# A gated delta rule kernel with its diagonal 8x8 blocks inverted on GpSimd, denser q and k tiles, and a rewritten order of work

## The chip, the cores and the metric

One core of a Trainium2 chip runs the whole program. The metric is the device time of one execution in microseconds (us), the median of the runs shown. Lower is better. TensorE is called PE here, VectorE DVE, ScalarE ACT, GpSimd POOL and SyncE SP, as the profile calls them.

## What is computed

The reference is one block of a network on x of 8 batches, 256 tokens and 256 features: a modulated layer norm, a gated delta rule attention with 32 heads, a gated feed forward, then a second modulated layer norm and a mixture of 8 experts. Nearly all of the time goes to the attention, cut here to what matters:

```python
q = short_conv(h @ Wq, conv_q_w).reshape(b, t, H, DK)    # H = 32, DK = 48
k = short_conv(h @ Wk, conv_k_w).reshape(b, t, H, DK)
v = short_conv(h @ Wv, conv_v_w).reshape(b, t, H, DV)    # DV = 96
q, k = (l2norm(q), l2norm(k))
g = -jnp.exp(A_log) * jax.nn.softplus(h @ Wa + dt_bias)
beta = jax.nn.sigmoid(h @ Wb)
def step(S, inp):                                        # over the tokens
    qt, kt, vt, gt, bt = inp
    S = S * jnp.exp(gt)[..., None, None]
    mem = jnp.einsum('bhk,bhkv->bhv', kt, S)
    delta = (vt - mem) * bt[..., None]
    S = S + jnp.einsum('bhk,bhv->bhkv', kt, delta)
    return (S, jnp.einsum('bhk,bhkv->bhv', qt * scale, S))
gate = (h @ Wg).reshape(b, t, H, DV)
o = (rmsnorm(o, gnorm_w) * jax.nn.silu(gate)).reshape(b, t, VD) @ Wo
```

short_conv is a causal convolution of 4 taps for each feature, followed by silu.

## The kernel before

The program has three parts, one after the other: `prepare` (norms, decay factors, beta), `delta_rule` (the attention) and `experts`. The change touches `delta_rule`, and `prepare` a little.

**Items.** `delta_rule` works on 64 items: 8 groups of 4 heads (QH = 4) times 8 batches. An item has two chunks of 128 tokens (CH = 2), so 8 units (U = 8) of one head and one chunk. In a chunk the recurrence becomes a linear system with a unit triangular matrix of 128 by 128 for each unit; the kernel inverts that matrix and then solves with two rounds of refinement (REFINE = 2).

**Inversion.** Seven levels (LEVELS = 7) join blocks of 1, 2, 4, ... 64 to blocks of twice the size. A level has two halves g = 0, 1 of 4 units each. `merge1(l, g)` multiplies the transposed inverse so far (tile tn) with the matrix (tile b16) on PE (L521), and DVE masks the result (L711, tile w16). `merge2(l, g)` makes the next tn (PE L534, ACT L840) and the next inverse tt (PE L541, ACT L843). The first and the last level need no L534. All four matmuls of a half are 128x128 in bf16.

**Stages.** An item passes four turns. Stage A makes q, k, v (`qk`, `v`, `taps`), the gates, the row norms (`norms`, `gains`), the decays (`decays`: 8 scans of 128 on DVE, L734), the key tile (`keys`), and the triangular matrices (`scores` on PE, `decayed` on DVE, `negate` on ACT and POOL). Stage B is the inversion, in all 14 halves of a turn. Stage C is the solve (`w0`, then `residual` and `delta` in turn, `state_out`, `ks`), and its end (`gated`, `oT`, `wo`, `acc`) reaches into the next turn as stage D. In one turn A, B, C and D work on four different items.

**Order.** A turn has 15 slots. `slots` walks through them and calls, on every engine, the pieces in one written order: merge2 and merge1 of B, then the tables A_FIRST, C_AT, D_AT and A_AT. Each engine executes its own instructions in that order and waits on semaphores for the others. So an instruction that waits holds everything queued behind it on its engine. POOL has the squares, two power functions, the scaled key tile kqb, and two `affine_select` for each chunk. SP issues, for each item, a copy of h (tile hb, L491), the decays (L492) and the cumulative decays (L495), and once in 8 items the weights.

q and k lie in 4 tiles of 128 rows, in which each head of 48 takes 64 rows (the rest is zero), so that a head starts at row 0 or 64.

Of the kernel before, what the change touches and what calls it, by code (L numbers as in the profile page):

```python
# [14 lines left out]
TAPS = 4  # L15
# [6 lines left out]
QH = 4  # L22
# [3 lines left out]
VT = QV // P  # L26
STEPS = NQ * B
U = CH * QH
LEVELS = 7
# [12 lines left out]
C_ID, C_MASK, C_HEAD, C_IOTA = 0, P, P * (1 + LEVELS), P * (1 + LEVELS) + 2  # L42
C_COLS = C_IOTA + E
# [58 lines left out]
def prepare(nc, A, mem, scr):  # L102

    with ExitStack() as ctx:
# [32 lines left out]
        z_ps, absz_ok, u_ok, sp_ok, a_ok, eb_ok, beta_ok, bt_ps, bcum_ok = (  # L137
            sem(n) for n in ("z_ps", "absz_ok", "u_ok", "sp_ok", "a_ok", "eb_ok", "beta_ok", "bt_ps", "bcum_ok"))
# [6 lines left out]
        def _(sp):  # L145
# [18 lines left out]
            sp.wait_ge(a_ok, 1)  # L164
            for g in range(GROUPS):
                sp.dma_start(scr["a"][2 * g:2 * g + 2].rearrange("b h t -> h b t"),
                             tmp["a"][H * g:H * (g + 1), :].rearrange("h (b t) -> h b t", b=2)).then_inc(scr_st, 16)
# [41 lines left out]
        def _(pool):  # L209
            pool.memset(nh[:], -0.5).then_inc(half_ok, 1)  # L210
            pool.wait_ge(half_ok, 1)
            def turn(g):
# [31 lines left out]
        def _(v):  # L244
# [4 lines left out]
            v.tensor_copy(mem["id16"][:], const[:, C_ID:C_ID + P])  # L249
            v.tensor_copy(mem["mask"][:], const[:, C_MASK:C_MASK + LEVELS * P].rearrange("p (l n) -> p l n", l=LEVELS))  # L250
# [84 lines left out]
def delta_rule(nc, A, mem, scr):  # L335

    with ExitStack() as ctx:
# [41 lines left out]
        cj = sb("cj", [P, QH])  # L379
# [37 lines left out]

        C_AT = {0: [("w0", 0)], 1: [("residual", 0, 0)], 2: [("delta", 0, 0)], 3: [("residual", 0, 1)],
# [1030 lines left out]
```

## Time and profile before

| what | value |
|---|---|
| median of 3 runs | 2803.08 us (2802.49 to 2806.18) |
| the profiled execution, its own time | 2806.17 us |
| its span in the profile | 2804.3 us, 61239 instructions |
| PE busy | 2561.5 us, 91% |
| PE weight loads busy | 2142.8 us, 76% |
| DVE busy | 2278.5 us, 81% |
| ACT busy | 1757.5 us, 63% |
| POOL busy | 597.0 us, 21% |
| mean granted clock of PE | 0.969 |

The loop of `delta_rule` runs from about 131 us to 2475 us of the span. Shares over the whole span therefore mix the loop with the parts around it; the loop is better read in a window of its own. A run of matmuls is shown as busy until its last result has come out, while the next run may start earlier, so the busy time of PE is more than the time in which it could take no other work.

### The profile page before, as it was taken

How to read it: one execution, taken by the hardware profiler on the slowest of the kernel's cores; microseconds unless marked ns; L12 is line 12 of the kernel's file. 1: busy time of each engine (PE TensorE's matmuls, PEld its weight loads, DVE VectorE, ACT ScalarE, POOL GpSimd, SP SyncE). 2: the span in 40 equal slices, each digit the busy share in tenths (PEclk: the TensorE clock that was granted, in tenths of full speed). 3: DMA queues.
4: the chain of work that ended last, by engine and by line, in shares of the span. 5: the costliest groups of instructions: out<-in, count | busy, mean ns of one | idle time of the engine just before them, and what ended most of it. 6: DMA issues, size and time to landing. Idle time of an engine off the chain costs nothing. (4 is left out here: it accounts for less than half of the span.)

```text
span 2804.3 us, 61239 instructions
## 1 busy us (share of the span) xinstructions
PE 2561.5 (91%) x22496; PEld 2142.8 (76%) x22496; DVE 2278.5 (81%) x5647; ACT 1757.5 (63%) x4018; POOL 597.0 (21%) x733
## 2 busy tenths in 40 slices
PE   1279999999999999999999999999999999879997
PEld 0168888888888888888888888888888888746565
DVE  3469999999999999999999999999999999624444
ACT  1157777777777777777777777777777777622221
POOL 0022222222222222222222222222222222100000
PEclk6589999999999999999999999999999999989998
DMA  2310011001100010002000200020002000030000
GB/s 92 94 41 28 14 45 41 28 15 32 54 25 18 23 50 28 28 8 64 28 28 2 71 28 28 2 71 28 28 2 71 28 28 1 1 114 26 12 24 15
DMA packets 93542, 95.34 MB, mean 34 GB/s; under 512 B 31217, under 2 KB 82106, under 8 KB 93250
## 3 DMA queue, kind: packets, MB, share of 16 engines
q1 hardware_dynamic: 93250, 91.44, 10.6%
q8 instruction: 184, 3.01, 0.4%
q14 instruction: 108, 0.88, 0.1%
HBM read 72.10 MB, written 2.54 MB: 27 GB/s over the span
## 5 line engine op out<-in xcount | busy, mean ns | idle before, releaser
L711 DVE TENSOR_TENSOR dr_w<-dr_ps,mask 128x512 bf16<-128x512 f32 x768 | 522.3, 680 | 175.3 <-PE dr_ps L521 175.2
L725 DVE SCALAR_TENSOR_TENSOR dr_y<-dr_ps,dr_cw,dr_y 128x255 f32<-128x255 f32 (+2 forms) x1344 | 573.0, 473 | 28.5 <-ACT dr_y L850 21.9
L840 ACT CAST dr_tn<-dr_ps 128x512 bf16<-128x512 f32 x640 | 374.9, 586 | 153.1 <-PE dr_ps L534 153.1
L843 ACT CAST dr_tt<-dr_ps 128x512 bf16<-128x512 f32 x768 | 460.5, 600 | 1.4 <-PE dr_ps L541 1.4
L625 PE MATMUL dr_ps<-dr_w,dr_am 128*128 128x96 f32 x3072 | 417.3, 279 | 2.5 <-ACT dr_w L902 2.5
L625 PEld LDWEIGHTS dr_ps<-dr_w,dr_am 128*128 128x128 f32 x3072 | 377.9, 192 | 10.5 <-ACT dr_w L902 3.0
L541 PE MATMUL dr_ps<-dr_tt,dr_w 128*128 128x128 bf16 x3072 | 297.9, 219 | 69.4 <-DVE dr_w L711 69.4
L521 PE MATMUL dr_ps<-dr_tn,dr_b 128*128 128x128 bf16 x3072 | 297.1, 219 | 0.0
L534 PEld LDWEIGHTS dr_ps<-dr_w,dr_tt 128*128 128x128 bf16 x2560 | 186.4, 98 | 141.3 <-issue 70.0
L547 PE MATMUL dr_ps<-dr_hb,dr_wqk 128*128 128x256 f32 x1024 | 255.8, 394 | 22.1 <-DMA dr_hb<-hT 22.1
L541 PEld LDWEIGHTS dr_ps<-dr_tt,dr_w 128*128 128x128 bf16 x3072 | 204.2, 98 | 81.3 <-DVE dr_w L711 80.6
L534 PE MATMUL dr_ps<-dr_w,dr_tt 128*128 128x128 bf16 x2560 | 249.0, 220 | 7.1 <-DVE dr_w L711 5.9
L944 POOL TENSOR_TENSOR dr_sq<-dr_qk 128x256 f32<-128x256 f32 x128 | 78.4, 612 | 718.2 <-ACT dr_qk L860 718.2
L734 DVE TENSOR_TENSOR_SCAN dr_dec<-dr_abc,const 128x128 f32<-128x128 f32 x512 | 223.5, 497 | 0.0
L547 PEld LDWEIGHTS dr_ps<-dr_hb,dr_wqk 128*128 128x128 f32 x1024 | 188.3, 194 | 43.7 <-issue 22.4
L767 DVE SCALAR_TENSOR_TENSOR dr_am<-dr_ps,dr_gam,dr_dec 128x256 f32<-128x256 f32 x512 | 216.8, 474 | 3.0 <-PE dr_ps L608 2.9
L968 POOL TENSOR_TENSOR dr_fo<-dr_vo,dr_nhalf 128x4 f32<-128x4 f32 x128 | 130.2, 1017 | 400.1 <-DVE dr_vo L805 400.1
L960 POOL TENSOR_SCALAR_AFFINE_SELECT dr_b<-dr_b 128x512 bf16<-128x512 bf16 x128 | 94.5, 738 | 546.2 <-ACT dr_b L892 546.2
L521 PEld LDWEIGHTS dr_ps<-dr_tn,dr_b 128*128 128x128 bf16 x3072 | 203.9, 98 | 0.0
L547 PE MATMUL dr_ps<-dr_hb,dr_wv 128*128 128x256 f32 x768 | 198.0, 394 | 0.8 <-DVE dr_y L725 0.8
L902 ACT COPY dr_w<-dr_ps 128x384 f32<-128x384 f32 x384 | 188.5, 491 | 12.0 <-PE dr_ps L625 11.9
L690 PE MATMUL dr_ps<-dr_wo,dr_oT 128*128 128x256 f32 x768 | 194.5, 390 | 1.0 <-ACT dr_oT L928 1.0
(187 smaller groups left out, 4688.8 us busy)
## 6 DMA issues: line engine op xcount, KB each, us to landing
dr_abc<-scr_a SPq DMA_DIRECT2D x64, 512.0 KB, 4.1
dr_hb<-hT SPq DMA_DIRECT2D x64, 256.0 KB, 2.5
dr_bcb<-scr_b SPq DMA_DIRECT2D x128, 64.0 KB, 3.3
ex_modb<-scr_mod SPq DMA_DIRECT2D x4, 1024.0 KB, 8.1
dr_wo<-in_Wo SPq DMA_DIRECT2D x1, 3072.0 KB, 11.3
dr_wv<-in_Wv SPq DMA_DIRECT2D x8, 384.0 KB, 4.1
dr_wg<-in_Wg SPq DMA_DIRECT2D x8, 384.0 KB, 4.0
p_x<-in_x SPq DMA_DIRECT2D x4, 512.0 KB, 6.3
```

The lines of the kernel that those rows point to most:

```text
L521: last = pe.matmul(ps[:, (X0, X1)[g], (u % QH) * P:(u % QH + 1) * P], b16[:, m, u, :], id16[:] if l == 0 else tn[:, u, :], start=True, sto ...
L534: last = pe.matmul(ps[:, (X2, X1)[g], (u % QH) * P:(u % QH + 1) * P], tt[:, u, :], w16[:, u, :], start=True, stop=True)
L541: last = pe.matmul(ps[:, (X0, X2)[g], (u % QH) * P:(u % QH + 1) * P], wt[:, u, :], id16[:] if l == 0 else tt[:, u, :], start=True, stop=True)
L547: last = pe.matmul(ps[:, bank, off:off + T], wt(k), hb[:, m, k, :], start=(k == 0), stop=(k == KT - 1))
L625: last = pe.matmul(ps[:, bank, h * DV:(h + 1) * DV], wt(h), x[:, h * DV:(h + 1) * DV], start=(start and h == 0), stop=(h == QH - 1), skip_ ...
L690: last = pe.matmul(ps[:, CO, 0:D], oT[:, t, :], wo[:, (it // B) * VT + t, :], start=(t == 0), stop=(t == VT - 1))
L711: v.tensor_tensor((tn if l == 0 else w16)[:, us, :], ps[:, (X0, X1)[g], :].rearrange("p (u n) -> p u n", u=QH), bc(mask[:, l, :], 1, QH), ...
L725: v.scalar_tensor_tensor(y[:, slot, x:T], ps[:, (A0, A1)[n % 2], off:off + T - x], cw[:, t, TAPS - 1 - x:TAPS - x], y[:, slot, x:T], ALU.m ...
L734: v.tensor_tensor_scan(dec[:, u, :], abc[:, m, h, c * P:(c + 1) * P], ident, 0.0, ALU.mult, ALU.add).then_inc(s["dec_ok"], 1)
L767: ins = v.scalar_tensor_tensor(am[:, m, u], ps[:, (A0, A1)[side], a * 2 * P:(a + 1) * 2 * P].rearrange("p (n t) -> p n t", n=2), gam[:, m, ...
L840: act.copy(tn[:, us, :], ps[:, (X2, X1)[g], :].rearrange("p (u n) -> p u n", u=QH)).then_inc(s["tn_ok"], 1)
L843: act.copy(dst, ps[:, (X0, X2)[g], :].rearrange("p (u n) -> p u n", u=QH)).then_inc(s["tt_ok"], 1)
```

## The change

1. **Inversion.** LEVELS goes from 7 to 4: the levels now start from blocks of 8. The inverses of the 8x8 diagonal blocks are made by forward substitution on POOL (`base`): one copy and 14 small dependent operations on 128 x (8 x 7 down to 8 x 1) elements. SP copies the diagonal 16x16 blocks of b16 into a dense tile (8 DMAs per item, `blocks`), PE spreads their rows with 14 bf16 matmuls of 64 columns (`rows`), ACT copies the result (128x448), POOL solves, and DVE expands the 8x8 results to full 128x128 tiles tt and tn (`expand`: a product, a 32x32 transpose and two products of 128x1024 in bf16). All levels but the last now make a new tn.
2. **Order.** The inversion starts at position 27 of an item's life (slot 12 of the second turn) and ends at 35 (slot 5 of the third); the solve starts at 36 (slot 6 of the third turn) where it started at 30. Slots 6 to 11 of a turn hold no merge, and `expand` lies in slot 11.
3. **Dense tiles.** q and k together take 3 tiles of 128 rows (KTL = 3) in place of 4. The convolution runs over 6 tiles in place of 7. After silu, SP moves the 8 heads to the old places by 10 DMAs per item (`heads_apart`). h is read in place, so the copy hb is gone.
4. **Scans.** The decay scans are 2 of 512 elements per item in place of 8 of 128. Their second input is now a diagonal times the gain gam, made on POOL (tile dg, two products of 128x512), so that the gain is in the decay. `decayed` is then 4 products of 128x512 in place of 8 of 128x256 with a scalar.
5. **Moved.** The scaling of the key tile goes from DVE to ACT (a copy) and POOL (`keys_scale`). The output norm factor is multiplied into the gate on POOL (2 products of 128x384 per item), and `gated` is 1 product of 128x384 per chunk in place of 4 of 128x96.

The core of the diff:

```diff
-LEVELS = 7
+BASE = 8
+LEVELS = 4
+LVL0 = 3
+M_FIRST = 27
+DEPTH = 4
...
+        FIRST = {3: [("silu", 0)], 5: [("silu", 1)], 7: [("silu", 2)], 11: [("negate", 0)], 13: [("negate", 1)]}
+        SOLVE = {36: [("w0", 0)], 37: [("residual", 0, 0)], 38: [("delta", 0, 0)], 39: [("residual", 0, 1)],
+                 40: [("delta", 0, 1)], 41: [("state_out",)], 42: [("ks",), ("mean", 0)], 43: [("w0", 1)],
+                 44: [("residual", 1, 0), ("gated", 0)], 45: [("delta", 1, 0), ("oT", 0)],
+                 46: [("residual", 1, 1), ("wo", 0)], 47: [("delta", 1, 1), ("acc", 0)], 48: [("out", 1)],
+                 49: [("mean", 1)], 51: [("gated", 1)], 52: [("oT", 1)], 54: [("wo", 1)], 55: [("acc", 1)]}
+        BLOCKS = {17: [("values", 0)], 18: [("round", 0)], 19: [("values", 1)], 20: [("rows", )], 21: [("base",)],
+                  26: [("expand",)]}
+        MAKE = {0: [("proj", 0)], 1: [("taps", 0, 0)], 2: [("taps", 0, 1), ("proj", 1)],
+                3: [("taps", 1, 0)], 4: [("taps", 1, 1), ("proj", 2)], 5: [("taps", 2, 0)],
+                6: [("taps", 2, 1), ("norms",)], 7: [("gains",), ("gate", 0)],
+                8: [("keys",), ("gate", 1)], 9: [("scores", 0), ("decays", 0)],
+                10: [("decayed", 0, 0), ("decayed", 0, 1), ("keys_scale",)], 11: [("scores", 1), ("decays", 1)],
+                12: [("decayed", 1, 0), ("decayed", 1, 1)]}
+        SLOTS = 15
...
+            for half in range(SLOTS):
+                at = [(st, half + SLOTS * k) for k, st in enumerate(stages) if st]
+                for st, x in at:
+                    k = x - M_FIRST
+                    if 0 < k <= 2 * LEVELS:
+                        on["merge2"](st, (k - 1) // 2, (k - 1) % 2)
+                    if 0 <= k < 2 * LEVELS:
+                        on["merge1"](st, k // 2, k % 2)
+                for table in (FIRST, SOLVE, BLOCKS, MAKE):
...
+            def expand(st):
+                it, m = st
+                v.wait_ge(s["xb_ok"], it + 1)
+                v.tensor_tensor(c32[:].rearrange("p u (r i) -> p u r i", r=4), bc(xb[:], 2, 4),
+                                bc(bc(const[:, C_QUART:C_QUART + 4], 1, U), 3, BASE), ALU.mult).then_inc(s["c32_ok"], 1)
+                v.wait_ge(s["c32_ok"], it + 1)
+                v.transpose(c32t[:].rearrange("p u i -> p (u i)"), c32[:].rearrange("p u i -> p (u i)")
+                            ).then_inc(s["c32t_ok"], 1)
...
+                v.tensor_tensor(tt[:].rearrange("p u (n i) -> p u n i", i=4 * BASE), bc(c32[:], 2, 4), blk,
+                                ALU.mult).then_inc(s["te_ok"], 1)
+                v.wait_ge(s["c32t_ok"], it + 1)
+                v.tensor_tensor(tn[:].rearrange("p u (n i) -> p u n i", i=4 * BASE), bc(c32t[:], 2, 4), blk,
+                                ALU.mult).then_inc(s["te_ok"], 1)
...
                 pe.wait_ge(s["rs_ok"], (it * 2 + 1) * REFINE)
+                pe.wait_ge(s["kg_ok"], it + 1)
...
+            def base(st):
+                it, m = st
+                n = it * (2 * BASE - 2)
+                wait(pool, s["c32_ok"], it)
+                pool.tensor_copy(xb[:], bc(const[:, C_UNIT:C_UNIT + BASE], 1, U)).then_inc(s["xs"], 1)
+                pool.wait_ge(s["ab_ok"], it + 1)
+                for j in range(BASE - 1):
+                    left = BASE - 1 - j
+                    pool.wait_ge(s["xs"], n + 2 * j + 1)
+                    pool.tensor_tensor(xt[:, :, 0:left], bc(xb[:, :, j], 2, left), ab[:, j, :, j + 1:BASE],
+                                       ALU.mult).then_inc(s["xs"], 1)
+                    pool.wait_ge(s["xs"], n + 2 * j + 2)
+                    ins = pool.tensor_tensor(xb[:, :, j + 1:BASE], xb[:, :, j + 1:BASE], xt[:, :, 0:left], ALU.add)
```

On POOL the order in a turn is, after the change: squares (slot 3), the scaling of the gate (4), `base` (6), then in slot 7 the two products dg, the square root of the norms and kqb, `keys_scale` (10), the selects (11 and 13) and again the scaling of the gate (12).

## Rows read from the trace of the kernel before

**Rows 1.** Busy time of each engine in one stretch of the loop (columns: stretch, length, PE, PEld, DVE, ACT, POOL, PEclk, DMA).
```profile
600.00:1000.00 400.00, 386.63 (x3750) 338.81 (x3748) 363.17 (x897) 291.47 (x674) 100.16 (x123) 1.00 0.11 33
```
**Rows 2.** Who waited for whom, whole span (total us, times, longest).
```profile
DVE dr_w L711 <- PE dr_ps L521: 175.2, 200, 3.6
```
**Rows 3.** Two lines of DVE (ns min/median/max, first and last start).
```profile
L734 DVE TENSOR_TENSOR_SCAN dr_dec<-dr_abc,const x512: 393/401/794, 138.8 to 2410.1; 128x128 f32<-128x128 f32 x171
...
L742 DVE TENSOR_SCALAR dr_kk<-dr_ps x64: 153/155/166, 149.0 to 2397.8; 128x8 f32<-128x8 f32 x64
```
**Rows 4.** Timeline of PE, single pieces (columns: start, us shown busy, instructions).
```profile
1005.99 1.46 PE L586 MATMUL dr_ps<-dr_wg,dr_hb 128*128 128x384 f32 x4
...
1007.28 0.39 PE L534 MATMUL dr_ps<-dr_w,dr_tt 128*128 128x128 bf16 x4
...
1007.51 0.39 PE L541 MATMUL dr_ps<-dr_tt,dr_w 128*128 128x128 bf16 x4
...
1010.31 1.08 PE L625 MATMUL dr_ps<-dr_w,dr_am 128*128 128x96 f32 x8
...
1011.23 1.49 PE L690 MATMUL dr_ps<-dr_wo,dr_oT 128*128 128x256 f32 x6
...
1019.99 1.96 PE L547 MATMUL dr_ps<-dr_hb,dr_wqk 128*128 128x256 f32 x8
```
**Rows 5.** Groups of DVE by form, 1000 to 1400 us (count, busy us, mean ns, idle before).
```profile
L711 DVE TENSOR_TENSOR dr_w<-dr_ps,mask 128x512 bf16<-128x512 f32 x134 | 91.1, 680 | 28.9 <-PE dr_ps L521 28.9
...
L725 DVE SCALAR_TENSOR_TENSOR dr_y<-dr_ps,dr_cw,dr_y 128x254 f32<-128x254 f32 x79 | 37.4, 474 | 0.4
L767 DVE SCALAR_TENSOR_TENSOR dr_am<-dr_ps,dr_gam,dr_dec 128x256 f32<-128x256 f32 x88 | 37.3, 474 | 0.0
...
L783 DVE TENSOR_TENSOR dr_r<-dr_rhs,dr_ps 128x384 bf16<-128x384 f32 x45 | 24.7, 548 | 5.0 <-PE dr_ps L625 5.0
L813 DVE SCALAR_TENSOR_TENSOR dr_og<-dr_ps,dr_fo,dr_gs 128x96 f32<-128x96 f32 x89 | 21.9, 307 | 0.0
```
**Rows 6.** Groups of DVE by form, 2400 us to the end.
```profile
L1368 DVE TENSOR_TENSOR ex_yo<-ex_yo,ex_x 128x1024 f32<-128x1024 f32 x4 | 4.9, 1226 | 0.1
```
**Rows 7.** Timeline, the handover from DVE to PE behind a mask.
```profile
1020.80 0.68 DVE L711 TENSOR_TENSOR dr_tn<-dr_ps,mask 128x512 bf16<-128x512 f32 x1
...
1021.78 0.39 PE L541 MATMUL dr_ps<-id,dr_tn 128*128 128x128 bf16 x4
```
**Rows 8.** Groups of ACT by form, 1000 to 1400 us.
```profile
L843 ACT CAST dr_tt<-dr_ps 128x512 bf16<-128x512 f32 x135 | 81.0, 600 | 0.0
L840 ACT CAST dr_tn<-dr_ps 128x512 bf16<-128x512 f32 x112 | 65.6, 586 | 26.0 <-PE dr_ps L534 26.0
```
**Rows 9.** Groups of POOL by form, 1000 to 1400 us.
```profile
L968 POOL TENSOR_TENSOR dr_fo<-dr_vo,dr_nhalf 128x4 f32<-128x4 f32 x23 | 23.4, 1017 | 64.6 <-DVE dr_vo L805 64.6
L950 POOL TENSOR_TENSOR dr_nrm<-dr_kk,dr_half 128x8 f32<-128x8 f32 x12 | 19.6, 1636 | 19.6 <-DVE dr_kk L742 19.6
L954 POOL TENSOR_TENSOR dr_kqb<-dr_qk,dr_bcb 128x256 f32<-128x256 f32 x24 | 17.0, 732 | 0.0
...
L944 POOL TENSOR_TENSOR dr_sq<-dr_qk 128x256 f32<-128x256 f32 x22 | 13.5, 612 | 119.6 <-ACT dr_qk L860 119.6
```
**Rows 10.** Timeline, the scans of the two chunks and POOL beside the first shown.
```profile
1014.40 2.14 DVE L734 TENSOR_TENSOR_SCAN dr_dec<-dr_abc,const 128x128 f32<-128x128 f32 x4
...
1014.73 0.84 POOL L960 TENSOR_SCALAR_AFFINE_SELECT dr_b<-dr_b 128x512 bf16<-128x512 bf16 x1 [8.01 <-ACT dr_b L892]
...
1026.76 1.36 DVE L734 TENSOR_TENSOR_SCAN dr_dec<-dr_abc,const 128x128 f32<-128x128 f32 x4
```
**Rows 11.** Busy time and granted clock in the second turn (columns as in the first group).
```profile
191.90:195.30 3.40, 1.34 (x18) 0.93 (x15) 3.40 (x8) 2.15 (x4) 0.72 (x2) 1.00 0.33 94
195.30:198.70 3.40, 3.32 (x19) 2.99 (x20) 1.96 (x5) 1.59 (x3) 1.22 (x2) 0.50 0.52 178
```
**Rows 12.** DMA issues by line (count, KB each, median us to landing).
```profile
dr_hb<-hT SPq DMA_DIRECT2D x64, 256.0 KB, 2.5
```

More of the change, by code:

```diff
@@ L26, with head_rows @@
 VT = QV // P
+QK = QH * DK
+KTL = 2 * QK // P
+def head_rows():
+    out = []
+    for n in range(2):
+        for h in range(QH):
+            at, end = n * QK + h * DK, n * QK + (h + 1) * DK
+            while at < end:
+                rows = min(end, (at // P + 1) * P) - at
+                out.append((n, h, at - n * QK - h * DK, at // P, at % P, rows))
+                at += rows
+    return out
+HEAD_ROWS = head_rows()
 STEPS = NQ * B
 U = CH * QH
-LEVELS = 7
+BASE = 8
[3 more added lines that the diff above has]
+DEPTH = 4
 REFINE = 2
@@ L423, in delta_rule @@
-        A_AT = {0: [("qk", 0)], 1: [("taps", 0, 0)], 2: [("taps", 0, 1), ("qk", 1), ("decays", 0)],
-                3: [("taps", 1, 0)], 4: [("taps", 1, 1), ("v", 0)], 5: [("taps", 2, 0)],
-                6: [("taps", 2, 1), ("norms",), ("v", 1)], 7: [("gains",), ("taps", 3, 0), ("gate", 0)],
-                8: [("keys",), ("gate", 1)], 9: [("scores", 0)], 10: [("decayed", 0, 0), ("decayed", 0, 1)],
-                11: [("scores", 1), ("decays", 1)], 12: [("decayed", 1, 0), ("values", 0)],
-                13: [("decayed", 1, 1), ("round", 0)], 14: [("values", 1)]}
@@ L449, in delta_rule @@
         PIECES = ("merge1", "merge2", "w0", "delta", "residual", "ks", "out", "state_out", "mean", "gated", "oT", "wo",
-                  "acc", "qk", "qk_silu", "v", "v_silu", "taps", "gate", "norms", "gains", "decays", "keys", "scores", "decayed", "negate",
+                  "acc", "rows", "base", "expand", "proj", "silu", "taps", "gate", "norms", "gains", "decays", "keys", "keys_scale", "scores", "decayed", "negate",
                   "values", "round")
@@ L569, in norms @@
+                for j in range(2):
+                    t = 2 * n + j
+                    for k in range(KT):
+                        wt = wqk[:, k, t * P:(t + 1) * P] if t < KTL else wv[:, k, (t - KTL) * P:(t - KTL + 1) * P]
+                        last = pe.matmul(ps[:, BANK[n], j * T:(j + 1) * T], wt, hT[:, k, (it % B) * T:(it % B + 1) * T], start=(k == 0),
+                                         stop=(k == KT - 1))
+                last.then_inc(s["pj_ps"], 1)
             def norms(st):
@@ L692, in wo_ @@
                 last.then_inc(s["wo_ps"], 1)
-            on.update(merge1=merge1, merge2=merge2, qk=qk_, v=v_, norms=norms, gate=gate, keys=keys, scores=scores,
+            on.update(merge1=merge1, merge2=merge2, rows=rows_, proj=proj, norms=norms, gate=gate, keys=keys, scores=scores,
                       values=values, w0=w0, residual=residual, delta=delta, out=outputs, state_out=state_out, ks=ks,
```

412 lines of the change are left out of this document (225 added, 187 removed).

## The prediction

> **What bounds the kernel now.** I read the busy time in a stretch of the loop first, since shares over the whole span mix in the parts around it. In 400 us PE is busy 387 us, DVE 363, ACT 291 and POOL 100, at a granted clock of 1.00 [rows 1]. The item's line L742 gives the turn: (2397.8 - 149.0) / 63 = 35.7 us [rows 3]. So a turn holds 34.5 us of PE as shown, 32.4 of DVE, 26 of ACT and 9 of POOL.
>
> Next, what of PE's time is real. Two runs of four bf16 matmuls start 0.23 us apart and are shown busy 0.39 us each [rows 4]: a matmul of 128 columns costs 0.056 us, and 0.16 us of each shown run is the last result coming out. By the same deduction a projection of eight instructions costs 1.75 us (L547), a gate chunk 1.3 (L586), a wo chunk 1.3 (L690) and a product of four heads in fp32 0.9 (L625) [rows 4]. Over the pieces of a turn this gives 33 us of PE that can't overlap. The waits agree: the largest wait of DVE is L711 for PE, 175 us, 2.7 us a turn [rows 2]. So PE (33) and DVE (32.4) are each nearly full, and about 2.7 us of 35.7 are lost because both execute one written order and hold each other up. The queue order matters as much as the sums.
>
> **The sums after the change, per turn.**
> - PE: merges go from 152 matmuls to 88, -64 x 0.056 = -3.6. One projection tile of seven goes, -0.87; norms -0.4 (12 small matmuls for 16, estimated at 0.11); `rows` adds 14 matmuls of 64 columns, below 0.056 each, +0.6. 33 becomes about 28.8.
> - DVE: six masks less, -6 x 0.68 = -4.1 [rows 5]. Three taps less, -1.4. `gated` goes from 8 x 0.31 to 2 x 0.55, -1.4; `decayed` from 8 x 0.47 to 4 x 0.68, -1.1; the keys leave, -0.6. The eight scans take 1.36 + 2.14 = 3.5 [rows 10]; two of 512 cost 1.1 to 1.36 each, because one element follows the other, about -1.1. `expand` is new. Its two products of 128x1024 lie between 0.68 (the rate of two elements in the time of one; nearest row L711, half as long) and 1.23 each (L1368, fp32) [rows 5, 6]; with the small product and the transpose, 2.0 to 3.2, and I take 2.5, about the middle, since the form isn't in the trace. 32.4 becomes about 25.
> - ACT: ten copies of 0.59 less [rows 8], some small work gone, two copies added: about 20.
> - POOL: the two dg products (two inputs, 512 elements) cost up to twice kqb's 0.73, I take 1.3 each; the gate scalings about 1.0 each; the key scaling 0.7 [rows 9]. For each of `base`'s 14 operations the rows give bounds: 0.61 for 256 elements, so 0.08 for the mean of 32 if the time were all per element, and above that a fixed part between 0 and 0.4 (1.64 - 1.02 = 0.62 us for four elements more of the power, so 1.02 has 0.4 fixed) [rows 9]. `base` lies between 1.3 and 7 us; with 0.2 of fixed part and handover I take 4. POOL has 9 + 2.6 + 2.0 + 0.7 + 4 = 18 us.
>
> No engine sum exceeds 29. If sums decided, the turn would fall by 4 to 6 us. They don't, and this is the step on which I depend.
>
> **The walk through the new order.** Before, each slot held a merge, which gives PE and DVE equal work. Now slots 6 to 11 have none, and DVE gets `expand`, the 512 scan and the state copy in one slot. I follow the loop of dependencies from PE's `merge2(0,1)` in slot 14 to the same instruction a turn later.
>
> Stretch 1, PE in order from there to `scores(0)` in slot 9: 72 merge matmuls 4.0, three projections 5.25, two gates 2.6, two wo 2.6, four residuals 3.6, the second output 1.55, scores 1.0, three deltas and a w0 0.7, the transposes 1.5, norms 1.3, rows 0.6. Sum 24.7 us. DVE can't prepare stretch 3 meanwhile: its queue stands at `decayed(0)`, which needs these scores.
>
> Stretch 2, scores to S: `delta(0,1)` 0.2, ACT's copy of w 0.5, the state product 0.5, three handovers 0.5. Sum 1.7.
>
> Stretch 3, DVE's queue from the state copy: copies 0.75, `expand` 2.5, scan 1.15, mask 0.6, the ks subtraction 0.46, `mean` 0.65, two `decayed` 1.25, mask 0.65: 8.0 us (an operation starts some 0.08 before its predecessor's shown end: four scans of 0.40 take 1.36 [rows 3, 10]). PE has only about 2.7 us of work beside it, in pieces that wait for these results, and its next instruction needs the last mask. Handover to a weight load behind a mask: 1021.78 - 1021.48 = 0.3 [rows 7].
>
> That is 24.7 + 1.7 + 8.0 + 0.3 = **34.7 us without one stall in stretch 1**. This floor moves with `expand` from 34.2 to 35.4.
>
> Stalls in stretch 1. (a) `norms`: the second projection ends 5.7 us of PE work before PE comes to norms, but its chain is ACT copy 0.85, taps 1.2, mask 0.65, mean 0.68, values 0.5, taps 1.2 on DVE, then two silus and a square 1.6, and handovers 0.6: 7.4. (Each is a count of operations at the rates of these groups [rows 5, 8], less the 0.08 of overlap; silu and square I take at 0.4 for 256 elements.) Stall 1.8. (b) The first merges and `oT(0)` behind DVE: 0.8. (c) `gate(1)` needs the bank that ACT reads, and little is queued between now: 0.5. Sum 3.1.
>
> (d) A wait is added: `state_out` waits for kg_ok. What is queued behind it on PE is the output product, scores(1), the first merge and ks; DVE's copy of S waits for it. On POOL, kg stands behind `base`, dg x2 2.6, nrm 1.64, kqb 1.46 and itself 0.7, that is 6.4 after `base`. `base` starts when ACT has copied the rows, behind silu(1), 0.6 us before norms can start; the state product could start 10 us after that. With `base` 4: 10.4. Stall 0.4; each us of `base` above 3.6 adds one us to the turn.
>
> Turn: 34.7 + 3.1 + 0.4 = **38.2 us**, 2.5 more than now. For 62 full turns +155. Around the loop: 8 fewer small weight DMAs and no copy of h (2.5 us to landing [rows 12]), against a later store of the decays and six more slots of drain; I take 0, bounds -10 and +10. The heads' 10 DMAs are hidden: the last three land, at the 2.5 us of L491 behind 1.8 of issue, about when `keys` is reached; if a us late, the turn grows by that us. The 8 DMAs of blocks have five slots of cover. The profiled execution took 2806.2, 3 above the median 2803.1; so 2806 + 155 = 2961, for the median **2958 us**.
>
> **A rule weighed.** The first scans run beside POOL's select and take 2.14 us for four, the others, alone, 1.36 [rows 10]: 0.39 for each of two held scans. By the Trainium skill, page "SBUF — State Buffer", section "SBUF: two separate sides", the shared port pair is an exclusive lock between GpSimd and a VectorE operation with two SBUF inputs, held for the whole instruction. The row agrees in sign and size. It speaks against this change, which doubles POOL's work and gives DVE three more operations of that kind: by it the turn could be 39.8, by the walk alone it is 38.2.
>
> **The rivals.**
> - *The port.* Five operations of DVE per turn (two scans, three of `expand`) have two SBUF inputs; four lie in stretch 3. At 0.4 each [rows 10] the turn is 39.8 and the time 3058. For it: POOL is busy half of the turn. Against: by my walk it is idle when `expand` runs. (Its page is the one just named.) 8%.
> - *The clock.* PE has 4 us of work in 11 us of stretches 2 and 3. In the second turn now, a stretch of 3.40 with PE busy 1.34 us was followed by one at a granted 0.50, that is 1.2 GHz in place of 2.4 [rows 11]. If this happens in every turn and the slow stretch falls on the start of stretch 1, 3.4 us give 1.7 us of work: turn 39.9, 3064. Against: the loop now is at 1.00, and the place can shift. 20%.
> - *POOL's chain.* `base` at 7 us adds 3: 41.2, 3144. 7%.
> - *The other side: faster.* The stalls of stretch 1 vanish since ACT and DVE slide ahead where I let them wait. It decides at 1.0 us: with stalls below that, 34.7 + stalls is under 35.7. With none and a short `expand`, 34.2: 2710; the middle of the case is 34.9, 2755. For it: now only 2.7 us are lost in a fuller turn. Against: the chain behind norms has 1.8 us more than PE has work. 25%.
> - *Nothing.* 35.6 to 35.8 us: 5%. This includes that the parts don't save what they say, for instance a scan of 512 that costs as much as four of 128.
>
> **How the numbers follow.** The walk 35%, slower: its own range is 36.9 to 39.4, 2877 to 3032. Port, clock and POOL, slower too: 35%. Faster 25%, nothing 5%. A measurement of this kernel can tell about 0.2% from no change. The range goes from 2725 (all of the faster case but its lowest tail) to 3110 (all but most of POOL's case). So faster 0.25, same 0.05, slower 0.70.
>
> **What would show it.** In the changed profile: a turn by L742's successor of 38.2; PE below 80% and DVE below 72% of a loop window; the largest waits being PE's first merge for te_ok and `merge2(0,1)` for its mask; a wait of norms for ACT's square. `expand` about 2.5 us, `base` about 4. The prediction fails if PE waits less than 5 us a turn, if `base` is over 5 or DVE's two-input operations stretch beside POOL, or if the granted clock is below 0.98 in the loop.

## The result and the profile after

| | before | after |
|---|---|---|
| median of 4 runs each | 2802.78 us | 3124.66 us (3124.19 to 3127.57) |
| ratio to before, 95% interval | | 1.1148 [1.1129, 1.1167] |
| span of the profiled execution | 2804.3 us | 3122.2 us |
| mean granted clock of PE | 0.969 | 0.871 |

The changed kernel is 11.5% slower: 322 us. The forecast was 2958 with a range up to 3110, so the direction was right, the size was not, and the time lies 15 us outside the range.

The page of after, its busy times and the granted clock in 40 slices of the span:

```profile
span 3122.2 us, 53272 instructions
...
PE 2577.8 (83%) x18784; PEld 2069.2 (66%) x18784; DVE 1969.4 (63%) x4176; ACT 1429.2 (46%) x3314; POOL 1187.9 (38%) x2027
...
PEclk6679988888888998888888888888888888879998
```

One eighth of the instructions is gone, DVE is busy 309 us less, ACT 328 less, and the program is longer. The row to see is PEclk: 8 in nearly every slice of the loop. A stretch of the loop as in [rows 1] (columns: stretch, length, PE, PEld, DVE, ACT, POOL, PEclk, DMA, GB/s), and the source line of `gains`, as in [rows 3]:

```profile
600.00:1000.00 400.00, 341.88 (x2707) 285.17 (x2705) 271.60 (x564) 203.47 (x479) 179.50 (x307) 0.88 0.14 31
```
```profile
L828 DVE TENSOR_SCALAR dr_kk<-dr_ps x64: 156/159/167, 143.6 to 2697.8; 128x8 f32<-128x8 f32 x64
```

In 400 us PE has 45 us less than in [rows 1] and DVE 92 less. (2697.8 - 143.6) / 63 = 40.5 us for a turn, where [rows 3] gave 35.7. Most turns of the steady loop (49 of 59) are 40.96 to 41.02 us long. Below, "a turn" is the mean of 59 turns of the loop between starts of this line (before 35.75, after 40.79), and "half-clock time" is what of a turn ran at a granted clock of 0.50.

Who waited for whom after the change, whole span (total us, times, longest):

```profile
DVE dr_r L857 <- PE dr_ps L691: 465.1, 254, 5.4
DVE dr_w L778 <- PE dr_ps L585: 350.5, 377, 3.9
...
PE dr_ps L598 <- DVE dr_w L778: 143.8, 130, 1.5
```

DVE's wait for its mask has doubled [rows 2], and its wait for the residuals of the solve is new in size. PE waits for DVE too. Both wait for each other: no engine is full.

**One turn by its stretches.** The order in time is: the pieces from the state copy to `merge2(0,1)` (here up to about 1001), then the long run of PE, the norms at 1022, gates and scores, and the state copy of the next turn at 1034.8:

```profile
996.00:1000.90 4.90, 2.28 (x24) 1.69 (x24) 4.83 (x8) 1.48 (x3) 1.29 (x2) 1.00 0.00 0
1001.00:1007.90 6.90, 6.19 (x42) 6.00 (x43) 3.06 (x6) 4.28 (x10) 2.01 (x3) 0.51 0.06 5
1008.00:1018.00 10.00, 10.00 (x95) 9.21 (x94) 7.05 (x16) 6.18 (x16) 0.54 (x1) 1.00 0.02 1
1018.00:1024.80 6.80, 5.18 (x54) 4.76 (x53) 5.67 (x14) 4.73 (x12) 4.37 (x11) 1.00 0.23 53
1024.90:1028.30 3.40, 3.40 (x13) 1.80 (x11) 0.94 (x5) 1.45 (x5) 2.85 (x10) 0.50 0.74 141
1028.30:1042.00 13.70, 10.03 (x79) 7.30 (x78) 10.47 (x18) 4.15 (x9) 8.17 (x8) 1.00 0.08 19
```

Two stretches of each turn of 40.96 us, together 10.2 us, run at a granted 0.50, that is 1.2 GHz in place of 2.4. The first follows 4.9 us in which PE was busy 2.28, and but for its first 0.7 us it lies on work that PE does without a pause. The second lies wholly on such work and follows the wait before the norms:

```profile
1022.33 1.48 PE L641 MATMUL dr_ps<-const,dr_sq 128*128 128x8 f32 x12 [1.62 <-ACT dr_sq L944]
```

Eight of the 59 turns have nearly the same waits and yet only 5.0 to 5.9 us at half clock, and they take 39.1 to 40.0 us. The next turn after the one above is of this kind: its 4.9 us are as poor in PE work as those above, and the clock stays at 1.00 behind them.

```profile
1037.00:1041.90 4.90, 2.28 (x24) 1.70 (x24) 4.83 (x9) 1.48 (x3) 1.30 (x2) 1.00 0.02 3
1042.00:1048.00 6.00, 4.98 (x49) 4.41 (x50) 3.15 (x6) 4.34 (x10) 2.14 (x4) 1.00 0.05 3
```

So such a place brings its stretch in most turns, not in all.

The end of the turn, where DVE sets the pace (timeline; start, us, instructions, idle before):

```profile
1034.78 0.73 DVE L864 COPY dr_S<-dr_ps 64x192 f32<-64x192 f32 x2
...
1035.54 0.43 DVE L784 TENSOR_TENSOR dr_c<-dr_xb,const 128x256 bf16<-128x256 f32 x1
...
1036.00 0.45 DVE L787 STREAM_TRANSPOSE dr_c32t<-dr_c 128x256 bf16<-128x256 bf16 x1
1036.37 0.65 DVE L791 TENSOR_TENSOR dr_tt<-dr_c,bd 128x1024 bf16<-128x1024 bf16 x1
1036.42 1.09 POOL L1044 TENSOR_SCALAR_AFFINE_SELECT dr_am<-dr_am 128x512 f32<-128x512 f32 x1
1036.94 1.12 DVE L794 TENSOR_TENSOR dr_tn<-dr_c32t,bd 128x1024 bf16<-128x1024 bf16 x1
1037.98 1.21 DVE L820 TENSOR_TENSOR_SCAN dr_dec<-dr_abc,dr_dg 128x512 f32<-128x512 f32 x1
...
1038.12 0.40 PE L585 MATMUL dr_ps<-dr_tn,dr_b 128*128 128x128 bf16 x4 [1.50 <-DVE dr_tn L794]
...
1042.90 0.40 PE L598 MATMUL dr_ps<-dr_w,dr_tt 128*128 128x128 bf16 x4 [1.50 <-DVE dr_w L778]
...
1043.65 0.64 POOL L1044 TENSOR_SCALAR_AFFINE_SELECT dr_am<-dr_am 128x512 f32<-128x512 f32 x1
```

From the state copy (1034.78) to `merge2(0,1)` (1042.90) it is 8.12 us; the expansion (L784 to L794) takes 2.52. PE waits 1.50 us for DVE twice here, and 0.75 us once between them (before `merge2(0,0)`, at 1039.98). One of the two products of one form takes 0.65 us and the other 1.12, while POOL's select beside it takes 1.09 where the same select takes 0.64 at 1043.65.

### The profile page after: what moved, and what is told of

The parts are those of the page before. It is cut to its first block and busy times, and to the rows that moved or that the text cites. A ratio compares the mean times of both kernels' runs of the same rounds, so it can differ in the third digit from the quotient of the medians.

```text
span 3122.2 us, 53272 instructions
## 1 busy us (share of the span) xinstructions
PE 2577.8 (83%) x18784; PEld 2069.2 (66%) x18784; DVE 1969.4 (63%) x4176; ACT 1429.2 (46%) x3314; POOL 1187.9 (38%) x2027
## 5 line engine op out<-in xcount | busy, mean ns | idle before, releaser
L778 DVE TENSOR_TENSOR dr_w<-dr_ps,mask 128x512 bf16<-128x512 f32 x512 | 353.3, 690 | 352.8 <-PE dr_ps L585 350.5
L808 DVE SCALAR_TENSOR_TENSOR dr_y<-dr_ps,dr_cw,dr_y 128x255 f32<-128x255 f32 (+2 forms) x1152 | 477.1, 472 | 24.8 <-ACT dr_y L924 24.8
L857 DVE TENSOR_TENSOR dr_r<-dr_rhs,dr_ps 128x384 bf16<-128x384 f32 x256 | 141.9, 554 | 465.1 <-PE dr_ps L691 465.1
L910 ACT CAST dr_tn<-dr_ps 128x512 bf16<-128x512 f32 x384 | 224.4, 584 | 221.5 <-PE dr_ps L598 221.0
L924 ACT ACTIVATE dr_y<-dr_ps,dr_cw 128x256 f32<-128x256 f32 x384 | 161.0, 470 | 255.7 <-PE dr_ps L630 255.7
L652 PE MATMUL dr_ps<-dr_wg,hT 128*128 128x384 f32 x512 | 276.1, 678 | 0.7 <-ACT dr_gs L950 0.7
L630 PE MATMUL dr_ps<-hT,dr_wqk 128*128 128x256 f32 x768 | 215.3, 422 | 22.8 <-DMA dr_cw<-in_conv_v_w 21.9
L913 ACT CAST dr_tt<-dr_ps 128x512 bf16<-128x512 f32 x384 | 229.1, 597 | 0.0
L630 PEld LDWEIGHTS dr_ps<-hT,dr_wqk 128*128 128x128 f32 x768 | 161.6, 227 | 45.1 <-issue 23.9
L630 PE MATMUL dr_ps<-hT,dr_wv 128*128 128x256 f32 x768 | 187.0, 380 | 2.4 <-DVE dr_y L808 2.4
```

The source lines that it names most:

```text
L630: last = pe.matmul(ps[:, BANK[n], j * T:(j + 1) * T], wt, hT[:, k, (it % B) * T:(it % B + 1) * T], start=(k == 0), stop=(k == KT - 1))
L652: last = pe.matmul(ps[:, A0, 0:QV], hT[:, k, at:at + P], wg[:, k, :], start=(k == 0), stop=(k == KT - 1))
L778: v.tensor_tensor(w16[:, us, :], ps[:, (X0, X1)[g], :].rearrange("p (u n) -> p u n", u=QH), bc(mask[:, l, :], 1, QH), ALU.mult).then_inc(s ...
L808: v.scalar_tensor_tensor(y[:, slot, x:T], ps[:, BANK[n], off:off + T - x], cw[:, t, TAPS - 1 - x:TAPS - x], y[:, slot, x:T], ALU.mult, ALU ...
L910: act.copy(tn[:, us, :], ps[:, (X2, X1)[g], :].rearrange("p (u n) -> p u n", u=QH)).then_inc(s["tn_ok"], 1)
L913: act.copy(dst, ps[:, (X0, X2)[g], :].rearrange("p (u n) -> p u n", u=QH)).then_inc(s["tt_ok"], 1)
```

## The experiments

The theory after this reading had two parts. **Order:** a turn is the walk through the written order, and the expansion in slot 11 stands on it. **Clock:** PE's low activity in the waits brings stretches at half clock, and these cost on top. Rivals: the low clock costs nothing, since PE waits anyway; and POOL's chain (`base`) sets the turn. The place of the expansion and the clock are tested first, alone and together.

### Expansion three slots earlier

```diff
-                  26: [("expand",)]}
+                  23: [("expand",)]}
```


> Changed kernel with one edit: expand stands at position 23 (slot 8) in place of 26 (slot 11), where DVE now idles 4.9 us waiting for a residual. Order theory (DVE's queue from the state copy to the mask of merge(0,1), 8.1 us, lies on the loop, expand's 2.5 us in it): the turn falls by 2.5 us, 3125 to about 2970. POOL theory (POOL's chain base, dg, nrm, kqb, kg sets the turn): no change, or slower if the port makes base longer. Clock theory alone (only the half clock costs): no change beyond what the clock does; half-clock time per turn would have to fall.

Measured: 2965.77 us, 1.0582 [1.0565, 1.0600], 159 us less than after; a turn of 38.30 with 7.1 us at half clock. PE's wait for `tn` before merge1(0,0) (1.50 us above) is gone, and so is the one of 0.75 before merge2(0,0). The wait for the last mask, before merge2(0,1), stays as it was:

```profile
1022.90 0.40 PE L598 MATMUL dr_ps<-dr_w,dr_tt 128*128 128x128 bf16 x4 [1.50 <-DVE dr_w L778]
```

This part of the order theory holds. Eight turns of this run had only 2.2 us of half-clock time, and these took 36.35 us. A line through all 59 turns gives 35.3 at no half-clock time: a first sign that clock and turn go together.

### Fillers: work for PE in its waits

The function `fill(n)` issues n bf16 matmuls of 512 columns whose result nobody reads; 20 per item, some 4.3 us of PE's time: 7 before merge1(0,0), 4 before merge2(0,0), 6 before the norms and 3 before state_out.

```diff
+            def fill(n):
+                for _ in range(n):
+                    pe.matmul(ps[:, X1, :], id16[:], mask[:].rearrange("p l n -> p (l n)"), start=True, stop=True)
...
...
+                        fill(7)
...
+                    fill(4)
...
+                fill(6)
...
+                fill(3)
```


> Changed kernel plus 20 matmuls of 512 columns in bf16 per item, whose results nothing reads, into a bank that is free in slots 6 to 13: 6 before norms, 3 before state_out, 7 before the first merge and 4 before the second, 4.3 us of PE work at full clock, nearly all in places where PE waits 0.6 to 1.6 us. Clock theory (half clock is granted 10.2 us per turn and each such us costs 0.31): the granted clock returns to 1.00 and the turn falls by up to 3.0 us, to about 2940. Rival (the low clock only falls where PE waits anyway and costs nothing): same time or up to 1 us per turn slower, 3125 to 3190.

Measured: 2914.01 us, 1.0389 [1.0372, 1.0406]. It is 211 us faster with more work, and nothing else is changed. A turn is 37.50 us, and 37.2 in those without half-clock time. The granted clock in the loop rose from 0.90 to 0.99 and the turn got shorter with more work in it. The rival that the low clock costs nothing is out.

### Both

> Both edits. If order and clock are two separate terms, they add: 3125 - 155 - 185 = about 2785, about the kernel before. If moving expand alone cures the clock, it is no faster than the first of the two alone, about 2970 or below; fillers that no longer find a wait would make it slower than 2785.

Measured: 2874.05 us, 1.0247 [1.0230, 1.0265]; 251 us less than after where the sum of the two is 370. All turns are 36.80 us long without half-clock time. So the clock was cured and the turn was still longer than expected. The trace shows where:

```profile
1026.09 1.69 PE L576 MATMUL dr_ps<-mask,id 128*128 128x512 bf16 x7
1027.61 0.39 PE L591 MATMUL dr_ps<-dr_tn,dr_b 128*128 128x128 bf16 x4
```

With the expansion early, PE does not wait before merge1(0,0) (L591 here), and the seven fillers now delay it. A smaller part of the missing 119 us was counted twice: the early expansion alone already lowers the half-clock time of a turn from 9.6 to 7.1 us. The same place in the kernel with the early expansion alone:

```profile
1017.62 1.14 PE L674 MATMUL dr_ps<-dr_qk 64*128 64x256 f32 x8
1018.69 0.40 PE L585 MATMUL dr_ps<-dr_tn,dr_b 128*128 128x128 bf16 x4
```

Filler work is free only in a wait that is still there.

### Without base

The inversion of the 8x8 blocks is left out: POOL copies the unit matrix, and the 14 small products and sums are not done.

```diff
-                for j in range(BASE - 1):
-                    left = BASE - 1 - j
...
-                    ins.then_inc(s["xb_ok"] if j == BASE - 2 else s["xs"], 1)
+                pool.tensor_copy(xb[:], bc(const[:, C_UNIT:C_UNIT + BASE], 1, U)).then_inc(s["xb_ok"], 1)
```


> Changed kernel without the 14 small operations of base on POOL (only its copy of unit rows stays, behind the same wait), so the 8x8 blocks are not inverted. POOL theory: POOL's chain gets 5.3 us shorter and the turn falls by 2 us or more, below 3000. Order theory: kg_ok comes at the same time as ACT's copy of w, so at most 0.3 us per turn, 3105 to 3125.

Measured: 3122.83 us (two executions), a turn of 40.75. POOL is busy 138 us of 400 in place of 178, and the time does not move. In this order POOL's chain hides completely.

### Fewer fillers, in the waits that are left

With the early expansion: 6 before the norms, 2 before state_out, 5 before merge2(0,1) into bank A1, none elsewhere.

```diff
+                if l == 0 and g == 1 and 5:
+                    pe.wait_ge(s["am_ok"], min(it + 2, STEPS) * 4)
+                    fill(5, A1)
```


> The expansion one turn's slot 8 (position 23) as before, and 13 filler matmuls instead of 20, only where the trace with the early expansion shows TensorE waiting: 6 before the norms (wait 1.6 us), 2 before state_out (0.6 us), 5 before merge2(0,1) (1.5 us, on bank A1), none before merge1(0,0) and merge2(0,0), where it doesn't wait. Clock-plus-order theory: over the turns of the run with the expansion alone, turn = 35.31 + 0.42 x half-clock us, so without half clock a turn is 35.3 us; the 20 fillers gave 36.80 at full clock since 7 to 11 of them (1.6 to 2.4 us) stood on the path. Against that run's 2874 a gain of 1.5 us x 62 = 92: 2782 us, ratio to before 0.992, faster than the kernel before. If the fillers left out were needed and one 3.4-us stretch at half clock per turn comes back: 36.7 a turn, 2870. If the residual rivals (port, GpSimd) set the turn and not the order, it stays at 2874.

Measured: 2806.46 us, 1.001 [1.0001, 1.0019]. All turns are 35.76 us long at full clock. The gain over the 20 fillers is 68 us where 92 were expected. The line through the turns of the early expansion alone gave 35.3 at no half-clock time; 0.45 us of that isn't reached. The reason is the added wait, seen below.

### Which place brings which low stretch

Fillers before the norms alone, and in slots 11 to 13 alone, in the changed kernel (expansion at 26).

> The changed kernel with 6 fillers per item before the norms alone, in a wait of 1.6 us. It tells which low stretch the granted clock answers to. If both places count for themselves (the 6.8 us at half clock behind the norms, the 3.4 us behind slots 10 to 14): the first goes, 3.4 us stay, turn 37.84 + 0.307 x 3.4 = 38.9, 3124.7 - 2.1 x 62 = 2995 us, clock about 0.94. If the slots 10 to 14 alone bring both: no change, 3120.

Measured: 3020.47 us, 1.0774 [1.0754, 1.0794] (three executions took 3019 to 3021 us; a fourth took 11187, which no trace explains); a turn of 39.18 with 6.6 us at half clock.

> The changed kernel with the 14 fillers of slots 11 to 13 alone (3 before state_out, 7 before merge1(0,0), 4 before merge2(0,0)), none at the norms. If both places count for themselves: 3.4 us at half clock go and 6.8 stay, turn 37.84 + 0.307 x 6.8 = 39.9, 3060 us, clock about 0.91. If the slots 10 to 14 alone bring both: about 37.5 a turn, 2915 us as with all 20.

Measured: 3048.35 us, 1.0874 [1.0856, 1.0892]; a turn of 39.62 with 5.5 us at half clock.

Each alone gives 104 and 76 us, both together 211. So both places count, but I had assigned them the wrong way round: with the norms filled, the 6.8 us stay and the 3.4 us go. They are not independent either: with the slots filled, 5.5 us stay and not 3.4. The trace of the run with the norms filled shows what comes ahead of the stretch that is left: 4.9 us with PE busy 2.66, in the slots 10 to 14.

```profile
993.80:998.70 4.90, 2.66 (x21) 1.82 (x21) 4.79 (x8) 0.89 (x2) 1.84 (x2) 1.00 0.01 3
998.80:1005.50 6.70, 5.49 (x45) 5.27 (x44) 4.04 (x9) 3.80 (x8) 3.03 (x4) 0.50 0.03 2
```

With the slots filled instead, all but one of the low stretches between 1000 and 1260 us begin 0.4 to 2.5 us after the norms' matmuls have begun.

The run with the norms filled has something better: two turns near its start (243.5 to 317.8) in which the changed order ran at full clock throughout.

```profile
243.50:317.80 74.30, 64.28 (x563) 52.55 (x564) 54.51 (x115) 41.43 (x99) 34.78 (x63) 1.00 0.13 30
```

Two turns are 74.3 us: 37.18 each (280.68 - 243.50). The fillers there lie in the wait before the norms and lengthen nothing: from the last work before them to the norms it is 1.62 us, as without them. Its marks, for the comparison with the walk:

```profile
259.58 0.40 PE L609 MATMUL dr_ps<-dr_w,dr_tt 128*128 128x128 bf16 x4 [1.50 <-DVE dr_w L791]
```
```profile
286.05 1.13 PE L686 MATMUL dr_ps<-dr_qk 64*128 64x256 f32 x8
...
296.76 0.40 PE L609 MATMUL dr_ps<-dr_w,dr_tt 128*128 128x128 bf16 x4 [1.50 <-DVE dr_w L791]
```
```profile
288.63 0.35 DVE L877 COPY dr_S<-dr_ps 64x192 f32<-64x192 f32 x1
```

So the clock costs 40.96 - 37.18 = 3.8 us of such a turn, for 10.2 us at half speed.

### Merges two slots earlier

The merges are spread over the slots in which PE has little to do, without any filler.

```diff
-M_FIRST = 27
+M_FIRST = 25
...
+                  23: [("expand",)]}
```


> The expansion at position 23 and the merges two slots earlier (first at 25, slots 10 to 14 and 0 to 3), no fillers. The solve stays at 36. Order theory: merges then lie in the slots where TensorE waits for VectorE and fill its gaps (0.6 and 1.5 us), but they put masks between the decayed products on VectorE, which delays scores(1) and the residuals. If the written order is what sets the turn, it moves by up to 1.5 us either way from 38.3: 2870 to 3060 us; a gain shows as a higher clock as well, since TensorE's gaps get smaller. If the clock's low stretch behind the norms is independent of it, 6.8 us at half clock remain.

Measured: 2849.94 us (2835.6 to 2857.3), 1.016 [1.0129, 1.0190], better than expected (2870 at best) and 116 us less than with the expansion alone. A turn is 36.40 with only 2.8 us at half clock, and 35.16 where it is 0.4; the 6.8 us of the last case did not stay. A line through the turns gives 35.25 us at no half-clock time, where that of the expansion alone gives 35.31. So the gain is the clock's: useful work in PE's gaps does what fillers do.

### The same with fillers, and one slot more

Merges at 25, 5 fillers before the norms, 2 before merge2(0,0), 5 before merge2(1,1), the merge of slot 14 in this order:

> Expansion at 23, merges from 25, and 12 fillers in the waits that the trace without fillers shows: 5 before the norms (1.35 us), 2 before merge2(0,0) (0.62 us), 5 before merge2(1,1) (1.50 us, bank A1, whose reader is by then done). Over the turns of the run without fillers the turn is 35.16 us where only 0.4 us stood at half clock. Clock theory: all turns go to 35.15 us at full clock; against the 35.76 us and 2806 us of the kernel with the merges at 27, 0.6 x 62 = 37 less: about 2768 us, ratio 0.987. If fillers stand on the path by up to 0.5 us a turn: 2800, ratio 0.998.

Measured: 2801.44 us, 0.9985 [0.9976, 0.9994], 35.64 us in most turns at full clock: the upper of the two values expected. Merges at 24:

> The same with the merges from 24 (slots 9 to 14 and 0 to 2) and 10 fillers (5 norms, 2 before merge2(0,0), 3 before merge2(2,0)). Order theory: one more slot of TensorE work beside the scores, one less beside the projections; the mask of merge(0,0) now stands before the keys' and scores' VectorE work. Expected within 1 us of a turn of 35.2: 2705 to 2830; it tells whether the turn still depends on the written order once the clock is full, or on TensorE's own work (then no change from the one at 25).

Measured: 2968.74 us, 1.0579 [1.0562, 1.0595], outside what I had expected. The trace shows a new wait:

```profile
1012.30 1.24 DVE L797 TENSOR_TENSOR dr_c<-dr_xb,const 128x256 bf16<-128x256 f32 x1 [1.44 <-POOL dr_xb L1087]
1013.58 0.45 DVE L800 STREAM_TRANSPOSE dr_c32t<-dr_c 128x256 bf16<-128x256 bf16 x1
1013.95 1.04 DVE L804 TENSOR_TENSOR dr_tt<-dr_c,bd 128x1024 bf16<-128x1024 bf16 x1
1014.91 0.68 DVE L807 TENSOR_TENSOR dr_tn<-dr_c32t,bd 128x1024 bf16<-128x1024 bf16 x1
```
```profile
1015.65 0.40 PE L591 MATMUL dr_ps<-dr_tn,dr_b 128*128 128x128 bf16 x4 [2.15 <-DVE dr_tn L807]
```

The first merge now stands one slot behind the expansion, and the expansion waits 1.44 us for the last operation of `base`. PE waits 2.15 us for both, and a turn at full clock is 37.95 in place of 35.64, 2.3 more. So by the trace POOL's chain is on the path here. No run of this order without `base` tests it.

Fillers before the norms alone, merges at 25:

> Expansion at 23, merges from 25, 5 fillers before the norms only. If the low stretches begin at the norms' wait in this order (the merges having closed the gaps of slots 10 to 12), these 5 alone bring the clock to 1.00: 35.2 a turn, 2770 us. If the wait of 1.5 us before merge2(1,1) counts for itself, about 3.4 us at half clock stay in part of the turns: 2790 to 2850.

Measured: 2806.03 us, 1.0005 [0.9996, 1.0014]; 35.16 us in turns without half-clock time, mostly 36.31 in those with 3.4. That is the second case. In the trace the stretches begin 0.2 to 1.4 us after the start of the merge2(1,1) that PE had waited 1.50 us for (1078.58 behind 1078.06, for one). The wait of 0.61 us before merge2(0,0) is there as well, and no run tells the two apart. 3.4 us cost 1.15 here.

### The last wait

In the run with merges at 25 and all fillers, those before merge2(1,1) started late and ended late:

```profile
1000.38 0.33 PE L703 MATMUL dr_ps<-dr_rhs,dr_tf 128*128 128x96 bf16 x4 [0.35 <-ACT dr_rhs L1009]
1001.83 1.03 PE L576 MATMUL dr_ps<-mask,id 128*128 128x512 bf16 x4 [1.13 <-DVE dr_am L856]
1002.70 0.39 PE L609 MATMUL dr_ps<-dr_w,dr_tt 128*128 128x128 bf16 x4
```

From L703 to L609 are 2.32 us; without fillers it was 1.83. The fillers waited for the last reader of their bank. (With the merges at 27 and 13 fillers the same two marks are 2.32 us apart as well. The 0.49 us more match the 0.45 by which that kernel missed 35.3.) Four of them into bank A0, free one product earlier (against the kernel with merges at 25 and all fillers; bank and number change together):

```diff
-                    pe.wait_ge(s["am_ok"], min(it + 2, STEPS) * 4)
-                    fill(5, A1)
+                    pe.wait_ge(s["am_ok"], min(it + 2, STEPS) * 4 - (it + 1 < STEPS))
+                    fill(4, A0)
```


> As the kernel with the merges at 25 and 12 fillers, but those before merge2(1,1) are 4 and go to bank A0, which VectorE has read one decayed product (0.7 us) earlier. In the trace of the 12 fillers a turn is 35.64 at full clock because the five wait 1.13 us for the last decayed product and end 0.5 us after merge2(1,1) could have begun; the run with fillers before the norms alone has turns of 35.16 where none of it stood at half clock. Order-and-clock theory: 35.16 a turn at full clock, 2801.4 - 0.48 x 62 = 2771 us, ratio 0.988, faster than both kernels. If four and not five fillers let the clock fall in part of the turns: up to 2806.

Measured: **2771.01 us, 0.9883 [0.9866, 0.9899]**: 1.2% faster than the kernel before and 354 us faster than the changed kernel. The turn is 35.16 in most cases, all at full clock. The same place:

```profile
1024.95 0.33 PE L703 MATMUL dr_ps<-dr_rhs,dr_tf 128*128 128x96 bf16 x4 [0.31 <-ACT dr_rhs L1009]
1025.59 1.04 PE L576 MATMUL dr_ps<-mask,id 128*128 128x512 bf16 x4 [0.30 <-DVE dr_am L856]
1026.78 0.40 PE L609 MATMUL dr_ps<-dr_w,dr_tt 128*128 128x128 bf16 x4 [0.16 <-DVE dr_w L791]
```

From L703 to L609 are 1.83 us again. The fillers start 0.64 us after L703 in place of 1.45; a fifth would have cost some 0.2 of these 0.8 us, so most of the gain is the bank's. The loop of it as in [rows 1]:

```profile
1000.00:1400.00 400.00, 380.50 (x3257) 302.57 (x3255) 319.17 (x655) 238.62 (x561) 211.94 (x358) 1.00 0.15 35
```

All runs in one table (a turn and half-clock time in us, means of 59 turns):

| kernel | time | turn | of it at half clock |
|---|---|---|---|
| before | 2803 to 2806 | 35.75 | 0 |
| after (expansion 26, merges 27) | 3124.7 | 40.79 | 9.6 |
| without base | 3122.8 | 40.75 | 9.5 |
| fillers in slots 11 to 13 | 3048.4 | 39.62 | 5.5 |
| fillers before the norms | 3020.5 | 39.18 | 6.6 |
| 20 fillers | 2914.0 | 37.50 | 0.8 |
| expansion 23 | 2965.8 | 38.30 | 7.1 |
| expansion 23, 20 fillers | 2874.1 | 36.80 | 0 |
| expansion 23, 13 fillers | 2806.5 | 35.76 | 0 |
| expansion 23, merges 24, 10 fillers | 2968.7 | 38.34 | 0.9 |
| expansion 23, merges 25 | 2849.9 | 36.40 | 2.8 |
| the same, 5 fillers | 2806.0 | 35.83 | 1.7 |
| the same, 12 fillers | 2801.4 | 35.73 | 0 |
| the same, 11 fillers, bank A0 | 2771.0 | 35.23 | 0 |

## Why the prediction was wrong

**What failed is the sum of the turn, 34.7 + 3.1 + 0.4: it has no term for the clock.** The prediction named the clock only as a rival of 20%, which added 1.7 us to the walk for one stretch of 3.4 us per turn, and left it out of the forecast since the loop of before is at 1.00. The runs show that it is a term of every turn beside the walk. In a turn of 40.96 us there are 10.2 us at half clock, and they cost 3.8 us (against 37.18 at full clock). Over 62 turns that is up to 234 us, more than all of the walk's 155. The sign was there in [rows 11]. The size was missed in two ways. I counted one place, stretch 3, and not the wait ahead of the norms, for which I had even predicted the stall; and behind stretch 3 there are 6.8 us, where I had taken 3.4. The evidence against it, that the loop of before is at 1.00 [rows 1], says nothing about an order in which PE is idle 58 us of 400 and not 13, that is 5.9 us of a turn and not 1.2.

The price of one us at half clock was taken too high, at 0.5. Measured: 3.8 / 10.2 = 0.37 in the changed kernel, 2.0 / 6.6 = 0.30 with the norms filled, 2.4 / 5.5 = 0.44 with the slots filled (39.62 against the 37.2 of the 20 fillers), 1.15 / 3.4 = 0.34 with the merges at 25, and 39.59 against 37.95 with 3.4 us, 0.48, with the merges at 24. Of the 10.2 us, 0.7 lie on a wait of PE, where they cost nothing, and a run of four merge matmuls starts 0.42 us after the one before, where it is 0.22 at full clock. What makes the rest of the difference, and why the price differs from run to run, was not tested.

**The walk**, against the turn at full clock (marks 259.58, 286.05 + 1.13, 288.63, 296.76 above):

| step | predicted | measured at full clock |
|---|---|---|
| stretch 1 with its stalls | 24.7 + 3.1 = 27.8 | 287.18 - 259.58 = 27.6 |
| stretch 2, scores to S | 1.7 | 1.45 |
| stretch 3 and handover | 8.0 + 0.3 | 8.13 |
| kg stall | 0.4 | none |
| turn | 38.2 | 37.18 |

So the working on which I said I depend was 1.0 us too long, and no row of the table is off by more than 0.4. Inside the first row that is luck: PE waits 1.9 us in it and not 3.1, and has 25.7 us of work and not 24.7. The stalls (b) and (c) were the error, 0.1 and 0.2 us in place of 0.8 and 0.5. The walk's error hid a part of the clock's: 2958 - 1.0 x 62 + 3.8 x 62 = 3132, against 3125 measured (not all turns have 10.2 us at half clock).

**Point by point.**
- *Expansion 2.5 us:* 2.52, and this too is luck: 0.47 of it is the port (below), and without that it would be near the lower bound of 2.0. Its place on the path is shown: moved three slots ahead it gives 159 us, part of it through the clock.
- *Norms stall 1.8:* PE waits 1.62 us for L944, the square on ACT. The terms given for that chain add up to 7.28 and not 7.4, which makes the stall 1.6 by its own working.
- *base 4 us:* 4.6, from 1022.68 to 1027.28. Each of its operations takes 0.22 to 0.31 us, with 0.30 to 0.39 from start to start. It costs nothing (3122.8 without it), so the rival of POOL's chain is excluded for the order of the change. With the merges at 24 it is real, by the trace.
- *kg stall 0.4:* the keys are ready at 1033.75, the solution w at 1033.90, a tie.
- *Scans 1.1 to 1.36 us:* 1.35 in the mean, 1.21 alone.
- *dg products 1.3 us each:* 1.04; *kqb* went from 0.73 [rows 9] to 1.00.
- *Outside the loop 0:* a kernel with turns of 35.76 has 2806.5, that of before with 35.75 has 2804.2, measured beside it. Right.
- *The port:* it is seen. L794 takes 1.12 and not 0.65 beside the select, which takes 1.09 and not 0.64. "Idle when `expand` runs" was wrong for POOL. The Trainium skill, page "SBUF — State Buffer", section "SBUF: two separate sides", gives an exclusive lock between the two for such operations, and whichever starts first holds it; the order of starts agrees. L791 began at 1036.37 and kept its 0.65, the select began at 1036.42 and took 0.45 more, L794 began at 1036.94 beside the select and took 0.47 more. The rival's price of 1.6 us on top of the walk didn't appear: the walk's own 2.5 for the expansion, taken from the middle of wide bounds, already holds the 0.47. No run takes the select away from beside the expansion.
- *What would show it:* DVE below 72% (68%) was right, PE below 80% was not (85% as shown; a run at half clock is shown busy longer). The condition under which I said the prediction fails, a granted clock below 0.98 in the loop, is met at 0.88 and 0.90, and so is the one on operations of DVE that stretch beside POOL (0.65 to 1.12).

**Why the change is slower at all.** Its parts do save: with the expansion at 23, the merges at 25 and PE kept at full clock, the same parts give 2771. The order of the change loses 1.4 us per turn to before at full clock (37.18 against 35.75) and up to 3.8 by the clock. That the remaining gain is only 35 us, where the engine sums allowed 4 to 6 us per turn, is not settled: PE shows 380 of 400 us busy in the last version, 11 fillers per item among them, and DVE 319.

## What to carry to other kernels

Lengths of waits on PE are not the whole price of a poor order: price the clock as a term that adds, count every place in the turn where PE has little work, and take the 0.3 to 0.5 us per us at half clock of these runs as a first estimate. When work is removed from slots, move what is left into them (merges from 25: 116 us); where a wait remains, matmuls without use may stand in it, as many as fit and into a bank whose reader is done. An operation of DVE behind which PE waits should go where both queues have slack, but not so late that its consumer stands right behind it.

## What the runs showed of the hardware

- More work made the kernel 211 us faster: 20 matmuls of 512 columns per item, in waits, took the granted clock in the loop from 0.90 to 0.99 (0.871 to 0.961 over the span).
- The waits ahead of a low stretch were short: with merges at 25 and only the norms filled, PE waited 1.50 us before merge2(1,1) and less than that elsewhere in the turn, and about half of the turns had 3.4 us at half clock; four fillers in it and two before merge2(0,0) removed them all.
- The same half-clock time has different prices by where it falls: with the norms filled, turns with 6.8 us each alternate between 38.71 and 39.80 us, where a turn at full clock is 37.18.
- Operations of DVE and POOL that overlap hold each other up, the later one each time: 0.65 to 1.12 us, and 0.64 to 1.09. A bf16 product of 128x1024 that isn't held takes 0.65, no more than one of 128x512 from fp32 (0.69).
